# Fillings behind all scatters, three experts' weights split by GpSimd, and waits for single experts

## The chip, the cores and the metric

The kernel runs on one core of a Trainium2 chip. The time is that of the device for one execution, in microseconds (us); lower is better. The inputs are fixed in shape, and each execution computes the whole output.

## The reference

`x` has 4 x 512 tokens of 256 numbers. Three steps are computed:

```
x = x + 0.5 * ffn(layernorm(x))
x = x + attention(layernorm(x))
x = x + 0.5 * ffn(layernorm(x))

ffn(t):   shared = silu(t @ shared_gate) * (t @ shared_up) @ shared_down      # 256 wide
          each token goes to the 2 best of 16 experts by its router logits
          routed = sum over the 2 of weight * (silu(t @ gate_e) * (t @ up_e)) @ down_e   # 128 wide
attention: 16 heads of 128; q, k, v and the output weights are codes times scales of blocks of 32
```

Both FFNs use the same weights. The results are close to those of float32: most factors are split into a high and a low part, and a product is three matmuls (high x high, high x low, low x high).

## The kernel before

**Stages.** The first FFN takes from 0 to about 175 us, the attention with 64 heads (4 batches x 16; head u is one of them) until about 925, the second FFN the rest. The five engines run five programs written out by hand (`sync_program`, `pool_program` for GpSimd, `act_program` for ScalarE, `dve_program` for VectorE, `pe_program` for TensorE). Each engine runs its instructions in the order of its program; semaphores are the only tie between them. So the order of the lines is the schedule.

**Experts.** Both FFNs sort the token rows by expert in a DRAM buffer `xs_dram[f]` (f is 0 or 1). Each expert has a region of 2048 + 128 rows. `to_experts` (L605 on) scatters the normalized rows, one indirect DMA of 128 rows at a time, issued by GpSimd: 4 blocks q of 512 tokens, 2 choices k, 4 tiles i, 32 scatters for an FFN. Blocks 0 to 2 count on semaphore `scat0`, block 3 on `scat_3`. A tile of 128 rows is then read back, two tiles (a pair p, 24 pairs) at a time. The last tile of an expert reaches past its rows; there must be finite numbers there, since they go through a transpose by a matmul. For FFN 0 one indirect DMA, the **filling** (L643), writes 16 rows from each partition, 128 rows behind each expert's last one, with whatever is in `R`; its index `fill` is made by `behind()` on VectorE. For FFN 1 there is no filling: during the attention SyncE writes zeros from `in_empty` over all regions of `xs_dram[1]`, in PIECES x NE = 64 writes (L453, `empty_piece`), one or two behind each head from head 3 on.

**Tile loads.** SyncE's `tile_loads` (L481 on) takes the row offsets of the tiles from a table `toff` that VectorE has computed, in groups of 1, 3, 4, 4, ... pairs, and issues two loads of 128 KB for each pair (L502). Each group's words are loaded into registers and checked against bounds (L492). The first FIRST_RUN = 4 pairs hold tiles that are full after blocks 0 to 2, so they wait for `scat0` alone; ahead of pair 4 SyncE waits for `scat_3`, and in FFN 0 for `empty` and `fill0` (L487 to L491).

**The tiles.** For pair p TensorE transposes pair p + 1 (L1818), then multiplies pair p with gate and up (`product`, L1712 to L1714; the expert's number is read from a word in a register), transposes the hidden rows of pair p - 1 (L1843) and multiplies pair p - 2 with the down weights. ScalarE and VectorE take the results out of PSUM (L886, L898, L903, L909; L1368, L1380, L1392). VectorE also makes tables between them: `shifts` at p = 0, `needs` at p = 1, `in_tiles` from p = 2.

**Weights.** The FFN's weights come in NCHUNK = 18 pieces of 768 columns: 2 of the shared expert, then 16 experts. SyncE loads piece c into one of STAGES = 4 buffers (`chunk`, L433) and waits before it until c - 3 splits are done; all of these loads stand before `tile_loads(0)` in its program. ScalarE copies the high part (`split_hi`, L868) and VectorE subtracts it for the low part (`split_lo`, L1190, counted by `w_lo`). In `pe_program` every pair of FFN 0 waits for all 18 splits before its first product. For FFN 1 the split weights are prepared again during the attention and come from DRAM (`w_dram`, semaphore `e_in`).

**Attention.** A head's probabilities are turned by two DMA transposes (L464, `flip`, the two halves of a head), issued by SyncE as soon as the planes are written; GpSimd casts the turned planes (L683), and TensorE multiplies them with the values (L1949 on). The same queue of SyncE carries the loads of weight parts (L479), the loads and the write-backs of experts' weights (L514, L519) and the zeros.

Of the kernel before, what the change touches and what calls it, by code (L numbers as in the profile page):

```python
# [5 lines left out]
P = 128  # L6
F32 = mybir.dt.float32
# [15 lines left out]
KT = D // P  # L23
# [30 lines left out]

RESULTS = 3
# [28 lines left out]
SLOW_FROM = 9  # L84

# [47 lines left out]
class Views:  # L133
# [4 lines left out]
    "cst_in rw_in rw tri b_in bo_in bo bias w_hi w_lo e_in dv av pool_steps "  # L138
# [4 lines left out]
    "tt row behind need there blank fill0 gpos empty scat0 scat_3 toff0 toff1 "  # L143
# [7 lines left out]
def build(nc, t):  # L151
    with ExitStack() as ctx:  # L152
# [44 lines left out]
        m.xs_words = m.xs_dram[0].rearrange("n (d w) -> (n d) w", w=1)  # L197
# [5 lines left out]
        m.any_rows = R[:, O_XT:O_XT + NT * D].bitcast(F32)  # L203
# [105 lines left out]
def chunk_place(m, c):  # L309

    if c < SH_CHUNKS:
        return [m.Wsh[:, l, c * CH:(c + 1) * CH] for l in range(2)]
    return [m.We[:, c - SH_CHUNKS, l, :] for l in range(2)]
# [94 lines left out]
PIECES = 4  # L408
# [17 lines left out]
def sync_program(nc, sp, t, m, s):  # L426
# [4 lines left out]
    def chunk(c):  # L431
        wait(sp, s["w_lo"], c - STAGES + 1)
        sp.dma_start(m.stg[c % STAGES], t["ffn_w"][:, c * CH:(c + 1) * CH]).then_inc(m.staged[c % STAGES], 16)  # L433
# [14 lines left out]

    def empty_piece(i):

        e, n = i // PIECES, P // PIECES
        r0, rows = e * REGION + i % PIECES * (REGION // PIECES), REGION // PIECES
        sp.dma_start(m.xs_dram[1][r0:r0 + rows, :].rearrange("(p a) d -> p (a d)", p=n),  # L453
                     t["empty"][0:n, :]).then_inc(s["empty"], 16)
# [26 lines left out]
    def tile_loads(f):  # L481
# [4 lines left out]
        for group in GROUPS:  # L486
            if done == FIRST_RUN:  # L487
                sp.wait_ge(s["scat_3"], 16 * TOPK * QB * (f + 1))
                if f == 0:
                    sp.wait_ge(s["empty"], 16)  # L490
                    sp.wait_ge(s["fill0"], 16)  # L491
            _, words = nc.values_load_multi_w_load_instructions(  # L492
                m.toff[0:1, done:done + group], engines=[SP_ENGINE], min_val=0, max_val=(1 << 18) - 1)
            for p, word in enumerate(words, done):
# [8 lines left out]
                if p >= STORE_AT:  # L503
                    store(f, p - STORE_AT)
                    if f == 0 and p in PART_AT:
                        part(PART_AT[p])
# [30 lines left out]
    pieces = iter(range(PIECES * NE))  # L537
    for u in range(UNITS):
# [14 lines left out]
        if u >= EMPTY_FROM:  # L553
            for _, i in zip(range(2 if u % 3 == 0 else 1), pieces):
                empty_piece(i)
# [46 lines left out]
def pool_program(nc, pool, m, s):  # L602
# [31 lines left out]
    for q in range(QB):  # L634
        pool.wait_ge(s["xn_act0"], QB * (q + 1) - 2)
        pool.wait_ge(s["xn_dve0"], 2)
        pool.wait_ge(s["pos0"], q + 1)
        to_experts(0, q, 0)
        if q == QB - 1:

            pool.wait_ge(s["behind"], 1)
            pool.wait_ge(s["xt_hi0"], KT * QB)
            nc.gpsimd.indirect_dma_start(  # L643
                out=m.xs_words, out_offset=bass.IndirectOffsetOnAxis(ap=m.fill[:, 0:1], axis=0),
                in_=m.any_rows, in_offset=None).then_inc(s["fill0"], 16)
        to_experts(0, q, 1)
# [113 lines left out]
    for t in range(1, UNITS + 1):  # L760
# [22 lines left out]
        if t == 60:  # L783
            positions(0)
            pool.wait_ge(s["posp"], 1)
            pool.wait_ge(s["empty"], 16 * (PIECES * NE + 2))
            scatters(0, range(2))
# [17 lines left out]
    to_experts(1, 3, 1)  # L805

# [27 lines left out]
def act_program(nc, act, t, m, s):  # L834
# [28 lines left out]
    split = iter(range(NCHUNK))  # L863
# [16 lines left out]
    def tiles(f):  # L880
        for p in range(-1, NPAIR + 2):
# [23 lines left out]
            if 0 <= p - 2:  # L905
                b = (p - 2) % RESULTS
                act.wait_ge(s["r_dn"], NPAIR * f + p - 1)
# [189 lines left out]
def dve_program(nc, dve, m, s):  # L1097
# [86 lines left out]
    split = iter(range(NCHUNK))  # L1184

    def split_lo(count):
        for _, c in zip(range(count), split):
            hi, lo = chunk_place(m, c)
            dve.wait_ge(s["w_hi"], c + 1)
# [286 lines left out]
    split_lo(2)  # L1476
    shared_lo(0, 1)
    positions(0, 3, K0)
    split_lo(2)
    counted(0, CNT)  # L1480
    behind()
    tables(0)
    shared_add(0, 0)
    tables_row(0)
    counted_first(CNT)
# [196 lines left out]
    tables_row(1)  # L1682
    counted_first(CNT)
# [34 lines left out]
def pe_program(nc, pe, m, s):  # L1718
# [83 lines left out]
    def tiles(f, word):  # L1802
# [3 lines left out]
        for p in range(-1, NPAIR + 2):  # L1806
# [13 lines left out]
            if 0 <= p < NPAIR:  # L1820
                b = p % 2
                es = [expert(2 * p + j) for j in range(2)]
                if f == 0:
                    pe.wait_ge(s["w_lo"], NCHUNK)
                elif p == 0:
# [348 lines left out]
```

## Time and profile before

| | us |
|---|---|
| median of 3 runs | 1073.38 (1072.83 to 1074.72) |
| the profiled execution, time | 1076.45 |
| the profiled execution, span | 1074.7 |
| TensorE busy | 979.0 (91% of the span) |
| VectorE busy | 798.6 (74%) |
| ScalarE busy | 674.9 (63%) |
| GpSimd busy | 626.8 (58%) |
| DMA | 216.64 MB, mean 202 GB/s |

The span is from the first to the last instruction of the profiled execution; its time has what lies around it too. The page cuts the span into 40 slices of 27 us, in tenths:

```profile
PE   5549999899999999999999999999999997589995
DVE  7758567888887777787777777777787887368545
POOL 1750348776436877667787576687636378630252
PEclk9759999999999999999999999999999999879997
DMA  9867652778678887999999999999954468946653
```

A digit is the busy share of an engine in a slice (9 is 90% or more), in the row PEclk the TensorE clock that was granted, in tenths of full speed. TensorE has open time at the beginning (slices 0 to 2), where the first FFN begins, and around slice 34, where the attention ends and the second FFN begins.

### The profile page before, as it was taken

The page shows a single profiled execution, that of the slowest core. Times are in us where ns is not written, and L with a number is a line of the kernel's source. Part 1 is how long each engine was busy: PE and PEld are TensorE (multiplying, and loading weights), DVE is VectorE, ACT ScalarE, POOL GpSimd, SP SyncE. Part 2 cuts the span into 40 slices and gives each one's busy share as a digit, 9 for nine tenths or more (in the row PEclk, how much of TensorE's full clock was granted, in tenths as well). Part 3 has the DMA queues.
Part 4 walks back from the last instruction along what each step waited for, and adds up shares of the span by engine and source line. Part 5 has one row for each costly group of instructions (what it writes and reads, how often), then busy time and mean ns, then how long its engine had stood idle before and what let it go on. Part 6 is the DMA issues. An engine that isn't in the chain of part 4 may idle for free. (4 is left out here: it accounts for less than half of the span.)

```text
span 1074.7 us, 18907 instructions
## 1 busy us (share of the span) xinstructions
PE 979.0 (91%) x5314; PEld 839.1 (78%) x5314; DVE 798.6 (74%) x1679; ACT 674.9 (63%) x1485; POOL 626.8 (58%) x915
## 2 busy tenths in 40 slices
PE   5549999899999999999999999999999997589995
PEld 4449987577888888888787887888888885479984
DVE  7758567888887777787777777777787887368545
ACT  5535644767776767777676776777767765135631
POOL 1750348776436877667787576687636378630252
PEclk9759999999999999999999999999999999879997
DMA  9867652778678887999999999999954468946653
GB/s 308 288 247 218 211 186 69 162 184 186 141 163 205 218 172 184 250 263 234 199 225 252 263 275 198 261 223 233 214 110 82 79 141 203 388 173 190 191 173 102
DMA packets 331797, 216.64 MB, mean 202 GB/s; under 512 B 274352, under 2 KB 315952, under 8 KB 330160
## 3 DMA queue, kind: packets, MB, share of 16 engines
q1 hardware_dynamic: 325104, 191.31, 70.5%
q0 software_dynamic: 6288, 18.88, 5.4%
q10 hardware_dynamic: 304, 5.24, 1.4%
q8 instruction: 46, 0.75, 0.3%
q14 instruction: 55, 0.45, 0.1%
HBM read 108.96 MB, written 80.48 MB: 176 GB/s over the span
## 5 line engine op out<-in xcount | busy, mean ns | idle before, releaser
L683 POOL CAST R<-turned 128x512 fp32r<-128x512 f16 x512 | 289.6, 615 | 216.4 <-DMA turned<-work 149.0
L1712 PE MATMUL bank<-R 128*128 128x512 f32 (+2 forms) x1056 | 390.7, 370 | 22.9 <-DVE R L1353 11.4
L1713 PE MATMUL bank<-R 128*128 128x512 f32 (+2 forms) x1056 | 379.7, 360 | 0.0
L1714 PE MATMUL bank<-R 128*128 128x512 f32 (+2 forms) x1056 | 379.0, 359 | 0.0
L1712 PEld LDWEIGHTS bank<-R 128*128 128x128 f32 x1056 | 204.9, 194 | 57.6 <-DVE R L1353 12.9
L1714 PEld LDWEIGHTS bank<-R 128*128 128x128 f32 x1056 | 204.6, 194 | 28.2
L1713 PEld LDWEIGHTS bank<-R 128*128 128x128 f32 x1056 | 205.3, 194 | 26.7
L985 ACT ACTIVATE bank<-bank,soft 128x512 f32<-128x512 f32 x256 | 170.1, 666 | 70.4 <-DVE soft L1525 63.5
L1518 DVE SCALAR_TENSOR_TENSOR R<-bank,bias,R 128x512 fp32r<-128x512 f32 x192 | 143.9, 750 | 67.9 <-ACT R L1005 41.4
L1525 DVE TENSOR_REDUCE soft<-bank 128x1 f32<-128x512 f32 x256 | 168.6, 686 | 25.4 <-PE bank L1714 25.2
L1539 DVE SCALAR_TENSOR_TENSOR work<-bank,soft,work 128x512 f16<-128x512 f32 x256 | 185.3, 743 | 2.3 <-ACT work L998 2.3
L998 ACT ACTIVATE work<-bank,soft 128x512 f16<-128x512 f32 x256 | 161.3, 682 | 16.2 <-DVE soft L1533 13.5
L617 POOL DMA_INDIRECT R<-y_tiles,gpos x48 | 46.7, 974 | 125.6 <-ACT work L909 64.7
L1949 PE MATMUL bank<-R 128*128 128x512 f32 x256 | 104.7, 409 | 10.3 <-POOL R L683 7.7
L1950 PE MATMUL bank<-R 128*128 128x512 f32 x256 | 101.0, 395 | 0.0
L1951 PE MATMUL bank<-R 128*128 128x512 f32 x256 | 100.4, 392 | 0.0
L1005 ACT ACTIVATE R<-bank,bias 128x512 fp32r<-128x512 f32 x64 | 44.1, 689 | 82.5 <-PE bank L1951 82.4
L979 ACT ACTIVATE R<-bank,bias 128x512 fp32r<-128x512 f32 x128 | 86.9, 680 | 0.0
L609 POOL DMA_INDIRECT xs_dram<-work,pos x48 | 51.0, 1062 | 48.5 <-DVE pos L1229 34.8
L1966 PE MATMUL bank<-R 128*128 128x256 f32 x256 | 72.2, 282 | 3.4 <-DVE R L1518 3.4
L1968 PE MATMUL bank<-R 128*128 128x256 f32 x256 | 72.4, 283 | 0.0
L1967 PE MATMUL bank<-R 128*128 128x256 f32 x256 | 72.4, 283 | 0.0
(163 smaller groups left out, 1375.9 us busy)
## 6 DMA issues: line engine op xcount, KB each, us to landing
xs_dram<-in_empty SPq DMA_DIRECT2D x64, 544.0 KB, 5.5
work<-in_parts SPq DMA_DIRECT2D x64, 256.0 KB, 4.2
work<-in_ffn_w SPq DMA_DIRECT2D x34, 384.0 KB, 4.9
work<-xs_dram SPq DMA_DIRECT2D x96, 128.0 KB, 2.6
y_tiles<-work SPq DMA_DIRECT2D x48, 256.0 KB
w_dram<-work SPq DMA_DIRECT2D x16, 768.0 KB, 4.7
R<-w_dram SPq DMA_DIRECT2D x16, 768.0 KB
y_tiles<-in_empty ACTq DMA_DIRECT2D x2, 2176.0 KB
```

The costliest lines, as they stand in the source:

```text
L683: nc.gpsimd.tensor_copy(whole_into(m, l, kb), whole_block(m, u, l, kb)).then_inc(s["cast_pool"], 1)
L985: nc.scalar.activation(s_bank(m, qb)[:], s_bank(m, qb)[:], ACT.Exp, bias=m.mx[:, qb:qb + 1], scale=1.0, accum_out=m.sm[:, qb:qb + 1]).then ...
L998: nc.scalar.activation(m.planes[:, qb, 0, :], s_bank(m, qb)[:], ACT.Copy, scale=m.ri[:, qb:qb + 1])\
L1518: v_.scalar_tensor_tensor(out=dst[:, 1, :], in0=bank[bk][:], scalar=m.bias[:, which, h:h + 1], in1=dst[:, 0, :].bitcast(F32), op0=ALU.add, ...
L1525: v_.reduce_max(m.mx[:, qb:qb + 1], s_bank(m, qb)[:], AX_X, negate=True).then_inc(s["max"], 1)
L1539: v_.scalar_tensor_tensor(out=m.planes[:, qb, 1, :], in0=s_bank(m, qb)[:], scalar=m.ri[:, qb:qb + 1], in1=m.planes[:, qb, 0, :], op0=ALU.m ...
L1712: nc.tensor.matmul(out, ah, bh, start=(i == 0 and first), stop=False)
L1713: nc.tensor.matmul(out, ah, bl, start=False, stop=False)
L1714: last = nc.tensor.matmul(out, al, bh, start=False, stop=(i == n - 1))
L1949: nc.tensor.matmul(bank[1][:], vh, ph, start=(kb == 0), stop=False)
L1950: nc.tensor.matmul(bank[1][:], vh, pl, start=False, stop=False)
L1951: ins = nc.tensor.matmul(bank[1][:], vl, ph, start=False, stop=(kb == QB - 1))
```

## The change

Four things are changed.

1. **Filling behind the scatters.** In FFN 0 the filling goes from between the scatters of block 3 behind all of them. In FFN 1 the 64 zero writes go; in their place GpSimd issues a filling of its own (`fill1`) behind the last scatter, when all experts' weights have landed (it takes its numbers from their place). SyncE waits for it ahead of pair 4, as in FFN 0. `behind()` on VectorE goes behind `tables_row`, and FFN 1 has one too.
2. **GpSimd splits three experts.** The pieces of steps 14, 16 and 17 of the loads (experts 13, 14, 15; steps 14 and 15 are exchanged) are split by GpSimd, a copy and a subtraction each, behind the filling of FFN 0. ScalarE and VectorE split the other 15; VectorE does 12 of them before the tables, where it did 14. In SyncE's loads, step c still waits for c - 3 splits.
3. **Waits for own experts.** In FFN 0 TensorE waits, for pairs 0 to 7, for the count of splits that the experts of its two tiles need (a wait against a register), and from pair 8 for all. ScalarE and SyncE get a wait each, since a staging buffer lies where they write.
4. **Checks.** The offsets that SyncE takes from the table are no longer checked against bounds.

```diff
+POOL_STEPS = (NCHUNK - 4, NCHUNK - 2, NCHUNK - 1)
+OWN_STEPS = tuple(i for i in range(NCHUNK) if i not in POOL_STEPS)
+CHUNKS = OWN_STEPS[:-1] + (NCHUNK - 3, NCHUNK - 4, NCHUNK - 2, NCHUNK - 1)
+SPLIT_BY = 8
...
-        m.xs_words = m.xs_dram[0].rearrange("n (d w) -> (n d) w", w=1)
+        m.xs_words = [xs.rearrange("n (d w) -> (n d) w", w=1) for xs in m.xs_dram]
-        m.any_rows = R[:, O_XT:O_XT + NT * D].bitcast(F32)
+        m.any_rows = [R[:, at:at + NT * D].bitcast(F32) for at in (O_XT, O_Z)]
...
 def chunk_place(m, i):
+    c = CHUNKS[i]
...
     def chunk(c):
         wait(sp, s["w_lo"], c - STAGES + 1)
-        sp.dma_start(m.stg[c % STAGES], t["ffn_w"][:, c * CH:(c + 1) * CH]).then_inc(m.staged[c % STAGES], 16)
+        sp.dma_start(m.stg[c % STAGES], t["ffn_w"][:, CHUNKS[c] * CH:(CHUNKS[c] + 1) * CH]).then_inc(m.staged[c % STAGES], 16)
...
                 sp.wait_ge(s["scat_3"], 16 * TOPK * QB * (f + 1))
-                if f == 0:
-                    sp.wait_ge(s["empty"], 16)
-                    sp.wait_ge(s["fill0"], 16)
+                sp.wait_ge(s["empty"], 32 if f else 16)
+                sp.wait_ge(s[f"fill{f}"], 16)
             _, words = nc.values_load_multi_w_load_instructions(
-                m.toff[0:1, done:done + group], engines=[SP_ENGINE], min_val=0, max_val=(1 << 18) - 1)
+                m.toff[0:1, done:done + group], engines=[SP_ENGINE], min_val=0, max_val=(1 << 18) - 1,
+                skip_runtime_bounds_check_because="the table ends at the spare tile")
...
                     if f == 0 and p in PART_AT:
+                        if PART_AT[p] == 0:
+                            sp.wait_ge(s["w_lo"], NCHUNK)
                         part(PART_AT[p])
...
-        if u >= EMPTY_FROM:
-            for _, i in zip(range(2 if u % 3 == 0 else 1), pieces):
-                empty_piece(i)
...
         to_experts(0, q, 0)
-        if q == QB - 1:
-
-            pool.wait_ge(s["behind"], 1)
-            pool.wait_ge(s["xt_hi0"], KT * QB)
-            nc.gpsimd.indirect_dma_start(
-                out=m.xs_words, out_offset=bass.IndirectOffsetOnAxis(ap=m.fill[:, 0:1], axis=0),
-                in_=m.any_rows, in_offset=None).then_inc(s["fill0"], 16)
         to_experts(0, q, 1)
+    pool.wait_ge(s["behind"], 1)
+    pool.wait_ge(s["xt_hi0"], KT * QB)
+    nc.gpsimd.indirect_dma_start(
+        out=m.xs_words[0], out_offset=bass.IndirectOffsetOnAxis(ap=m.fill[:, 0:1], axis=0),
+        in_=m.any_rows[0], in_offset=None).then_inc(s["fill0"], 16)
+
+    pool.wait_ge(s["w_lo"], len(OWN_STEPS))
+    for n, c in enumerate(POOL_STEPS):
+        hi, lo = chunk_place(m, c)
+        pool.wait_ge(m.staged[c % STAGES], 16 * (c // STAGES + 1))
+        nc.gpsimd.tensor_copy(hi, m.stg[c % STAGES]).then_inc(s["w_pool"], 1)
+        pool.wait_ge(s["w_pool"], n + 1)
+        nc.gpsimd.tensor_tensor(lo, m.stg[c % STAGES], hi.bitcast(F32), ALU.subtract).then_inc(s["w_lo"], 1)
...
-            pool.wait_ge(s["empty"], 16 * (PIECES * NE + 2))
...
     to_experts(1, 3, 1)
+    pool.wait_ge(s["behind"], 2)
+    pool.wait_ge(s["e_in"], 16 * NE)
+    nc.gpsimd.indirect_dma_start(
+        out=m.xs_words[1], out_offset=bass.IndirectOffsetOnAxis(ap=m.fill[:, 0:1], axis=0),
+        in_=m.any_rows[1], in_offset=None).then_inc(s["fill1"], 16)
...
-    split = iter(range(NCHUNK))
+    split = iter(OWN_STEPS)
...
+                if f == 0 and p == 2:
+                    act.wait_ge(s["w_lo"], len(OWN_STEPS))
...
     shared_mul(0, 1)
-    split_lo(2)
+    split_lo(1)
     shared_lo(0, 1)
     positions(0, 3, K0)
-    split_lo(2)
+    split_lo(1)
     counted(0, CNT)
-    behind()
     tables(0)
     shared_add(0, 0)
     tables_row(0)
+    behind()
     counted_first(CNT)
     split_lo(NCHUNK)
     tiles(0)
...
     tables_row(1)
+    behind()
     counted_first(CNT)
...
-                if f == 0:
+                if f == 0 and p < SPLIT_BY:
+                    for e in es:
+                        pe.wait_ge(s["w_lo"], pe.snap(e + (SH_CHUNKS + 1), min_val=SH_CHUNKS + 1, max_val=NCHUNK))
+                elif f == 0 and p == SPLIT_BY:
                     pe.wait_ge(s["w_lo"], NCHUNK)
-                elif p == 0:
+                elif f == 1 and p == 0:
                     pe.wait_ge(s["e_in"], 16 * NE)
```

## Rows read from the trace of the kernel before

**Rows 1.** Busy time in a stretch of the attention (clock, DMA share, GB/s last).

```profile
340.00:750.00 410.00, 407.25 (x1989) 342.08 (x1988) 319.85 (x535) 296.17 (x661) 298.31 (x460) 1.00 0.95 228
```

**Rows 2.** Timeline of SyncE's queue in the attention: start, us, what, count.

```profile
342.43 4.13 SPq L464 DMA_TRANSPOSE turned<-work  x2
...
571.38 1.21 SPq L453 DMA_DIRECT2D xs_dram<-in_empty  x2
574.35 9.06 SPq L464 DMA_TRANSPOSE turned<-work  x2
...
587.32 5.58 SPq L464 DMA_TRANSPOSE turned<-work  x2
...
599.19 4.95 SPq L464 DMA_TRANSPOSE turned<-work  x2
...
610.17 5.62 SPq L464 DMA_TRANSPOSE turned<-work  x2
...
788.13 4.76 SPq L464 DMA_TRANSPOSE turned<-work  x2
```

**Rows 3.** TensorE's timeline, first FFN: start, us, what [idle before <- what ended it].

```profile
73.74 1.11 PE L1818 MATMUL bank<-cst,work 128*128 128x128 f32 x4 [7.23 <-DMA work<-xs_dram]
...
83.48 0.38 PE L1712 MATMUL bank<-R 128*128 x1 [1.12 <-DVE R L1392]
...
84.34 0.60 PE L1818 MATMUL bank<-cst,work 128*128 128x128 f32 x4
```

**Rows 4.** Busy time from pair 4 to the end of the tiles.

```profile
84.00:146.00 62.00, 61.80 (x519) 60.53 (x518) 42.74 (x108) 37.50 (x86) 10.69 (x12) 1.00 0.64 196
```

**Rows 5.** GpSimd's timeline, first FFN: filling and last scatter.

```profile
62.39 3.30 POOL L643 DMA_INDIRECT xs_dram<-R,fill  x1 [0.30 <-issue]
...
69.79 0.96 POOL L609 DMA_INDIRECT xs_dram<-work,pos  x1 [0.30 <-issue]
```

**Rows 6.** The filling (L643): from its start to landing, min/median/max.

```profile
DMA to landing us min/median/max: 10.5/10.5/10.5
```

**Rows 7.** Busy time while the filling flows (DMA share, GB/s last).

```profile
66.00:76.00 10.00, 2.77 (x14) 2.37 (x13) 1.17 (x2) 1.69 (x3) 4.38 (x6) 0.50 0.96 342
```

**Rows 8.** SyncE's tile loads, pairs 0 to 3; landing of those until 92.

```profile
L502 SPq DMA_DIRECT2D work<-xs_dram x8: 3/644/1199, 63.3 to 70.6; - x8
...
DMA to landing us min/median/max: 2.1/4.0/7.6
```

**Rows 9.** VectorE's timeline, first FFN: the last four splits.

```profile
61.31 3.54 DVE L1190 TENSOR_TENSOR R<-work,R 128x768 fp32r<-128x768 f32 x4
```

**Rows 10.** SyncE's last four loads of weights, first and last start.

```profile
L433 SPq DMA_DIRECT2D work<-in_ffn_w x4: 328/328/328, 52.1 to 55.8; - x4
```

**Rows 11.** SyncE ahead of pair 4: the table's words, then the first loads.

```profile
L492 SPq TENSOR_LOAD <-toff x1: 317/317/317, 75.8 to 75.8; - x1
...
L502 SPq DMA_DIRECT2D work<-xs_dram x2: 333/334/336, 77.8 to 78.4; - x2
```

**Rows 12.** Groups by shape, GpSimd: the splits of experts' weights in the attention.

```profile
L700 POOL TENSOR_TENSOR work<-work 128x768 fp32r<-128x768 f32 x16 | 29.5, 1847 | 1.3
...
L698 POOL CAST work<-work 128x768 fp32r<-128x768 f32 x16 | 13.3, 829 | 0.0
```

**Rows 13.** Timelines of GpSimd and of VectorE around 156 us.

```profile
156.26 0.76 POOL L675 TENSOR_TENSOR R<-work,R 128x256 fp32r<-128x256 f32 x1
...
156.46 0.58 DVE L1166 SCALAR_TENSOR_TENSOR ln<-ln 128x4 f32<-128x4 f32 x1
...
157.46 0.16 DVE L1166 SCALAR_TENSOR_TENSOR ln<-ln 128x4 f32<-128x4 f32 x1
```

**Rows 14.** FFN 1: last scatter, SyncE's loads from pair 4, TensorE's pair 4.

```profile
958.71 0.96 POOL L609 DMA_INDIRECT xs_dram<-work,pos  x1 [0.31 <-issue]
...
L502 SPq DMA_DIRECT2D work<-xs_dram x3: 332/333/887, 964.1 to 965.2; - x3
...
974.94 0.49 PE L1818 MATMUL bank<-cst,work 128*128 128x128 f32 x3
```

More of the change, by code:

```diff
@@ L137 @@
 SEMAPHORES = (
-    "cst_in rw_in rw tri b_in bo_in bo bias w_hi w_lo e_in dv av pool_steps "
+    "cst_in rw_in rw tri b_in bo_in bo bias w_hi w_lo w_pool e_in dv av pool_steps "
     "pre_in pre_mul pre_out "
@@ L142 @@
     "lg0 lg1 lg_sb rk_sb l_read0 l_read1 hot0 hot1 e2 rank0 rank1 cnt pos0 pos1 posp "
-    "tt row behind need there blank fill0 gpos empty scat0 scat_3 toff0 toff1 "
[1 row of a table added]
     "gu silu h h_hi h_lo dn x_add "
@@ L306, with chunk_place @@
 TABLE = (COUNT[1], COUNT[1] + NPAIR + WORDS)
-def chunk_place(m, c):
+def chunk_place(m, i):
+    c = CHUNKS[i]
     if c < SH_CHUNKS:
@@ L407 @@
 EMPTY_FROM = 3
-PIECES = 4
 def part_of(kind, g, hh):
@@ L447, in sync_program @@
     sp.dma_start(m.xs_dram[0][SPARE:XROWS, :], t["empty"][:, 0:D]).then_inc(s["empty"], 16)
[L449 to L454, printed above, removed]
     def empty_spare():
@@ L536, in sync_program @@
     sp.wait_ge(s["sh_out"], 16)
-    pieces = iter(range(PIECES * NE))
     for u in range(UNITS):
@@ L1182, in xt_lo @@
             .then_inc(s[f"xt_lo{ph}"], 1)
-    split = iter(range(NCHUNK))
+    split = iter(OWN_STEPS)
     def split_lo(count):
@@ L1188, in split_lo @@
             hi, lo = chunk_place(m, c)
-            dve.wait_ge(s["w_hi"], c + 1)
+            dve.wait_ge(s["w_hi"], OWN_STEPS.index(c) + 1)
             v_.tensor_tensor(lo, m.stg[c % STAGES], hi.bitcast(F32), ALU.subtract).then_inc(s["w_lo"], 1)
```

1 row of the table SEMAPHORES is left out of this document.

## The prediction

> **What bounds the kernel now.** I read first the busy time by stretch. In most of the attention TensorE is busy 407.25 of 410 us at full clock, with the DMA engines 0.95 busy [rows 1], so only work that holds TensorE up counts there. I then took the DMA queue's own timeline, because each head starts with a DMA transpose. From the head that starts at 342.43 to the one that starts at 788.13 there are 40 heads, 445.7 us; a usual head takes 10.98 us (599.19 to 610.17), 40 of them 439.2 us. So 6.5 us are lost in these 40. They are lost in few places: behind 574.35 the next head comes after 12.97 us. There the transposes occupied the queue for 9.06 us, right behind two emptying writes at 571.38 [rows 2]. Five heads lose something (at 507, 574, 643, 688 and 755 us): 1.3, 2.9, 1.5, 0.6 and 0.2 us. In each the transposes occupy the queue for longer than usual, GpSimd's casts are late, and TensorE waits for them.
>
> The second place is the start of the first FFN's tiles, in TensorE's timeline. Pair 1 is transposed only at 73.74 after 7.23 us of waiting for its load; pair 4 at 84.34 [rows 3]. From there to 146 TensorE is busy 61.80 of 62 us [rows 4], so a start that comes earlier is kept to the end of the stage, and what follows hangs on that end. Why is pair 1 late? GpSimd issues the filling at 62.39, between the scatters of the last block, and four scatters follow until 70.75 [rows 5]. The filling lands 10.5 us after its start, at 72.9 [rows 6]; between 66 and 76 the DMA engines are 0.96 busy [rows 7]. The loads of pairs 0 to 3 are issued from 63.3 to 70.6 [rows 8] and land in that crowd.
>
> **The change, part by part.** *1. Filling behind the scatters (FFN 1).* The four scatters now come first: 62.39 + 4 x 1.265 = 67.45. The filling is generated 67.45 to 70.75 (3.30 us [rows 5]) and its data flow after that, no longer beside the loads of pairs 0 to 3.
>
> When are these loads issued? Two fewer splits precede the tables on VectorE, 2 x 0.885 us by the four that take 3.54, and the fill's index moves behind them; before, the table was ready just ahead of these four, at 60.9 [rows 9]; now it is some 2 us earlier. But SyncE gains nothing by it: its last two weight loads, at steps 16 and 17, wait for the 13th and 14th split. Before, these were done by 55.8 [rows 10]. Now they come behind the tables: I put the table at 58.9, 1.0 us of index and counts behind it, then two splits, until 61.7. Then come two weight loads, and the first tile load is at 63.4 to 64.3 (63.3 before), pair 1 some 1.5 us behind, at 65 to 65.8. Of the landing times the least is 2.1 and the median 4.0 [rows 8]; I take 3, as the only company are the two weight loads and scatters: pair 1 at 68.5, against 73.74. By that, TensorE would be at pair 4's place at 84.34 - 5.2 = 79.1.
>
> Pair 4's load waits for the filling. Its data now move alone: 2.1 MB at the rate of [rows 7], 342 GB/s, are 6.1 us, so it lands at about 76.9 (bounds: 76.0 at a faster rate, 77.95 by the 10.5 us of [rows 6]). Before, the release was at 75.8 and the first load at 77.8 [rows 11]; 2.0 us in which the table's words are loaded and checked. The change drops the checks: I take 0.7 (bounds 0.4 to 2.0). First load 77.6, second 0.6 behind, landed 2.1 to 3 later, 80.3 to 81.2: say 80.6. So the filling, not pair 1, becomes the last wait: a gain of 3.7 instead of 5.2.
>
> *2. GpSimd's three splits.* One costs 0.83 + 1.85 us [rows 12], three with their waits 8.4: from 70.8 to 79.3, on an engine that has then nothing to do until the first gather of results. They are in time: the pairs go through the experts in order, and 13 to 15 (first ready at 73.6, 76.4, 79.2) come in pairs 5 to 7, multiplied from 82 on. VectorE and ScalarE do three fewer, which were not last there.
> They do have company. Where GpSimd runs a two-input instruction of 256 columns at 156.26 until 157.02, VectorE's instruction with two SBUF inputs started at 156.46 takes 0.58 us, until 157.04, instead of the 0.16 of the same one at 157.46 [rows 13]: it waits until GpSimd's ends. In the new place three of 1.85 us run beside VectorE's `shifts` and `needs`, whose end releases pair 0's down product; that product was already 1.12 us late [rows 3], and TensorE reaches pair 4 right after it. A block moves the 79.1 out; its first 1.5 us are hidden by pair 4's load. I take 1.85 us (one instruction; bounds 0 and 3.7, two): some 0.3 us are lost, and pair 4 is at 81.0. **Parts 1 and 2: -3.4 us**, bounds -5.2 and -1.5.
> The Trainium skill, page "SBUF — State Buffer", section "Who interferes with whom", says that such a pair of instructions contends for one read interface; its summary says the second blocks until the first ends. The trace agrees with its 157.02 and 157.04; by the rule at its worst the parts give the -1.5 of the bound, without it -3.7.
>
> *3. Waits for the own experts.* TensorE waits twice for each of pairs 0 to 7. Alone it gains nothing, since VectorE reaches the tiles only behind its own splits (62.6); it is what keeps pair 0 from waiting for GpSimd's 79.3. The trace shows no register-valued wait of TensorE. A gain is excluded, since instructions are added alone; at the other end SyncE's handling of four words (2.0 us [rows 11]) gives 0.5 us for each of 16, 8 us if none was hidden. I take 0.1: pairs 0 to 3 wait for pair 4's load anyway, and behind them the queue is ahead of the array (61.80 of 62 [rows 4]).
>
> *4. No emptying in the attention.* 64 writes of 544 KB go, 35 MB, and with them most of the backlog ahead of the transposes; weight loads and write-backs of experts' weights stay. I take the whole 6.5 us less 0.1: **-6.4 us**. Bounds: -6.6, and -3.6 if the worst head kept its loss, since its 12.97 us stand right behind both kinds [rows 2].
>
> *5. Filling in FFN 2.* The last scatter is issued at 958.71 [rows 14]; the filling would follow at 960.0. It lands at 969.4 (3.3 + 6.1) to 970.5 (10.5). Before, pair 4's load went at 964.1 [rows 14]; now 0.7 behind the filling, 970.1 to 971.2, second 0.6 later, landed 2.1 to 3 later: 972.8 to 974.8. TensorE is at pair 4 at 974.94 [rows 14]. What hides it are pairs 0 to 3 and VectorE's `needs`, by 0.1 to 2.1 us. All weights must have landed too; they are issued before the last block's scatters. VectorE has three small instructions more (0.65 us) where it afterwards waits. I take **+0.1**, bounds 0 and +1.5.
>
> **Sum:** -3.4 + 0.1 - 6.4 + 0.1 = -9.6. The profiled execution took 1076.45 with a span of 1074.7; it becomes 1066.9 with a span of 1065.1. The median of the three runs is 1073.38; less 9.6 it is **1063.8 us**.
>
> **Rivals.** *A, locks and late loads eat FFN 1's gain.* VectorE's tables instructions meet two or three of GpSimd's 1.85 us, or pair 1 lands at 71: -1.5 instead of -3.4, with +1 in FFN 2 instead of +0.1: 1066.6. For it speaks [rows 13]; against it that pair 4's load hides a part. *B, the attention's late transposes are not due to the emptying.* Weight loads and write-backs stay in these heads: the 6.4 stay, 1070.2. For it: other heads stand behind two emptying writes and lose nothing; against it: the queue was longest occupied right behind a full load of all kinds, of which these writes are the largest part [rows 2]. *C, the change doesn't do what it says*: an early pair has an expert of GpSimd's and TensorE waits until 79.3 all the same. The first product, now at 74.4 (0.7 behind pair 1), comes 4.9 later: +4.9 - 6.4 + 0.1, 1072. Against it: tiles come in expert's order, eight of them before pair 4. *D, slower.* Both tile streams now stand at pair 4 until the filling lands. If each filling took d longer than the 10.5 us of [rows 6], FFN 1 would give d - 2.6 (landing at 77.95, pair 4 at 81.7), FFN 2 d - 0.1; with -6.4 from the attention the sum 2d - 9.1 is above +2.1 from d = 5.6 on; at d = 7 it is +4.9, 1078.3. Against it: that landing was measured in a crowd, and now the engines are idle around it.
>
> **Chances.** Forecast 0.66, A 0.15, B 0.11, C 0.04, D 0.04. A measurement of this kernel tells some 0.2% (2.1 us) from no change: faster 0.92 (forecast, A, B), same 0.04 (C), slower 0.04 (D). The forecast's own range is 1061.6 (-5.2 - 6.6) to 1066; the one for 8 in 10 takes in A and, for part 4's bound of -3.6 beside it, reaches to 1068.5, and below to 1060.5, since emptying writes stand behind heads ahead of 342 too, which I counted at nothing.
>
> **What the profile after would show.** Pair 1's transposes near 68.5 and pair 4's near 81, with the wait there on its load or on VectorE's L1392 before it; SyncE's last two weight loads near 61 and 62; GpSimd's splits ending near 79; all heads between 342 and 788 at 10.98 us and a DMA share clearly below 0.95; the second filling landing by 970.5 and no wait of TensorE at FFN 2's pair 4. Wrong would be: slow heads that remain, a filling that lands later than 78, or gaps between the products of pairs 4 to 7.

## The result and the profile after

| | before | after |
|---|---|---|
| median of 20 runs each, us | 1074.4 (1069.65 to 1077.15) | 1071.24 (1067.84 to 1074.66, one outlier of 3727.68 aside) |
| the profiled execution, time (span) | 1076.45 (1074.7) | 1067.94 (1066.1) |

The ratio of the times is 0.9969 (95% interval 0.9957 to 0.9981): **3.3 us faster, where 9.6 were predicted**, and outside the predicted range. The two profiled executions differ by 8.5 us. That overstates the change: the one of before is near the slowest of its 20 runs, that of after near the fastest of its own.

I call this chip A. The later runs were on three faster chips (before: medians of 1050.8, 1049.0 and 1050.2), together called B, but for the last three, on a chip like A (before: 1076.4), which goes as A too. Each ratio below is to before on the same chip.

The profile after, with the lines that answer to those of before. First the busy time by stretch, as in [rows 1], [rows 7] and [rows 4] (clock, DMA share, GB/s last):

```profile
340.00:750.00 410.00, 409.84 (x2014) 347.11 (x2013) 323.77 (x543) 300.68 (x671) 303.25 (x467) 1.00 0.74 166
66.00:76.00 10.00, 7.92 (x38) 7.17 (x38) 5.14 (x10) 4.12 (x7) 9.14 (x9) 0.62 0.83 319
84.00:146.00 62.00, 61.22 (x505) 59.58 (x505) 40.29 (x102) 36.65 (x85) 11.79 (x14) 1.00 0.67 202
```

The attention's DMA share has gone from 0.95 to 0.74, and TensorE's open time in these 410 us from 2.75 to 0.16. The timeline of SyncE's queue has the same 40 heads as [rows 2]:

```profile
340.24 4.78 SPq L463 DMA_TRANSPOSE turned<-work  x2
...
571.37 5.91 SPq L463 DMA_TRANSPOSE turned<-work  x2
...
582.35 4.74 SPq L463 DMA_TRANSPOSE turned<-work  x2
...
780.25 4.72 SPq L463 DMA_TRANSPOSE turned<-work  x2
```

The 40 heads take 440.01 us instead of 445.70, 10.98 from 571.37 to 582.35 and nearly so elsewhere. The first FFN in TensorE's timeline, as [rows 3]; then VectorE and GpSimd beside each other:

```profile
67.94 1.12 PE L1828 MATMUL bank<-cst,work 128*128 128x128 f32 x4 [0.79 <-DMA work<-xs_dram]
...
77.59 1.08 PE L1828 MATMUL bank<-cst,work 128*128 128x128 f32 x4 [2.83 <-DMA work<-xs_dram]
81.74 0.60 PE L1828 MATMUL bank<-cst,work 128*128 128x128 f32 x4
```

```profile
68.03 0.96 POOL L639 DMA_INDIRECT xs_dram<-R,fill  x1 [0.31 <-issue]
...
72.59 1.84 POOL L649 TENSOR_TENSOR R<-work,R 128x768 fp32r<-128x768 f32 x1
...
72.75 1.74 DVE L1269 SCALAR_TENSOR_TENSOR runs<-runs,tab 128x48 f32<-128x48 f32 x1
```

The view of the filling's line alone gives its landing, as in [rows 6]:

```profile
DMA to landing us min/median/max: 9.2/9.2/9.2
```

Pair 1 is 5.8 us earlier, pair 3 (the line of 77.59) waits 2.83 us for its load, and pair 4 is 2.6 us earlier, without a wait for its own load. VectorE's L1269 takes 1.74 us beside GpSimd's subtraction; it took 0.21 before. The filling lands 9.2 us after its start, at 77.3. Pair 3's two loads are issued at 68.21 and 69.62, so they are under way beside it.

In the second FFN TensorE waits before pair 1 and before pair 0's products, and the two waits are longer than before. The first windows are of that stretch in after, the last line is of before:

```profile
952.91 0.63 PE L1828 MATMUL bank<-cst,work 128*128 128x128 f32 x4 [1.85 <-DMA work<-xs_dram]
956.20 0.58 PE L1722 MATMUL bank<-R 128*128 x1 [2.66 <-issue]
...
969.62 0.60 PE L1828 MATMUL bank<-cst,work 128*128 128x128 f32 x4
```

```profile
954.00:958.00 4.00, 1.80 (x8) 1.81 (x9) 3.15 (x6) 2.68 (x5) 0.00 (x0) 0.54 1.03 344
958.00:962.00 4.00, 4.00 (x24) 4.00 (x23) 1.08 (x6) 0.38 (x1) 0.00 (x0) 0.61 0.49 154
```

```profile
962.00:966.00 4.00, 3.80 (x20) 3.80 (x21) 2.67 (x9) 1.08 (x3) 0.00 (x0) 0.62 0.40 108
```

From pair 0 to pair 4 it takes 19.2 us; before it was 16.0. The filling is issued at 950.90 and lands at 959.1; the DMA engines are full beside it, and TensorE, after its waits, has a clock of 0.54 and 0.61 (its lower level of 1.2 GHz is 0.5) until 962. Before had a slow stretch there too, 0.62 over four microseconds. The difference is mostly waiting: TensorE's waits of over half a microsecond between pairs 0 and 4 add up to 6.2 us, before to 3.8.

### The profile page after: what moved, and what is told of

Read it like the earlier page. It is cut to its first block and busy times, and to the rows that moved or that the text cites. A ratio compares the mean times of both kernels' runs of the same rounds, so it can differ in the third digit from the quotient of the medians.

```text
span 1066.1 us, 18770 instructions
## 1 busy us (share of the span) xinstructions
PE 982.0 (92%) x5314; PEld 845.6 (79%) x5314; DVE 797.4 (75%) x1679; ACT 672.8 (63%) x1482; POOL 633.8 (59%) x922
## 5 line engine op out<-in xcount | busy, mean ns | idle before, releaser
L994 ACT ACTIVATE bank<-bank,soft 128x512 f32<-128x512 f32 x256 | 170.3, 667 | 70.5 <-DVE soft L1534 67.1
L606 POOL DMA_INDIRECT xs_dram<-work,pos x48 | 50.1, 1044 | 49.0 <-DVE pos L1238 35.5
```

Of the source, the lines that this page charges most:

```text
L994: nc.scalar.activation(s_bank(m, qb)[:], s_bank(m, qb)[:], ACT.Exp, bias=m.mx[:, qb:qb + 1], scale=1.0, accum_out=m.sm[:, qb:qb + 1]).then ...
```

## The experiments

Stage times of all profiled executions, in us, read from the starts of TensorE's transposes (L1818 and its like) and of SyncE's transposes. "40 heads" is the stretch of [rows 2]; "heads 0 to 12" ends where it begins; "second start" is from pair 0 to pair 4 of the second FFN, "second rest" from pair 4 to pair 23.

| kernel | chip | pair 1 | pair 4 | pair 23 | heads 0 to 12 | 40 heads | second start | second rest |
|---|---|---|---|---|---|---|---|---|
| before | A | 73.7 | 84.3 | 138.4 | 154.0 | 445.7 | 16.0 | 54.6 |
| before_fourth | A | 73.7 | 84.7 | 138.4 | 154.4 | 446.5 | 16.6 | 54.4 |
| after | A | 67.9 | 81.7 | 136.4 | 153.7 | 440.0 | 19.2 | 54.3 |
| after_fourth | A | 79.5 | 90.3 | 143.9 | 154.3 | 440.5 | 18.8 | 55.0 |
| after8 | A | 68.4 | 81.1 | 136.4 | 154.5 | 439.8 | 18.8 | 54.4 |
| before_again | B | 68.8 | 80.0 | 133.2 | 153.4 | 445.7 | 13.6 | 53.2 |
| before_third | B | 71.5 | 82.3 | 135.5 | 154.1 | 444.1 | 13.6 | 53.2 |
| after_again | B | 66.6 | 81.8 | 135.4 | 155.4 | 440.0 | 13.6 | 53.2 |
| after_third | B | 66.7 | 79.1 | 133.9 | 155.7 | 440.5 | 13.7 | 53.3 |
| empt_only | B | 68.5 | 79.9 | 133.1 | 154.6 | 441.1 | 13.7 | 57.0 |
| ffn1_only | B | 66.3 | 78.5 | 132.7 | 155.7 | 447.6 | 13.7 | 53.2 |
| fill1_added | B | 70.7 | 81.2 | 134.4 | 153.9 | 445.9 | 15.0 | 57.0 |
| fill0_back | B | 71.5 | 81.3 | 134.9 | 155.3 | 441.8 | 13.7 | 53.5 |
| no_pool_split | B | 65.8 | 79.5 | 135.3 | 154.6 | 441.7 | 13.6 | 53.2 |
| empt_nocheck | B | 69.9 | 80.4 | 133.6 | 153.6 | 440.5 | 13.7 | 53.2 |
| empt_store8 | B | 69.1 | 80.0 | 133.2 | 153.7 | 439.4 | 15.6 | 54.9 |
| best8 | B | 70.5 | 81.2 | 134.4 | 153.6 | 440.5 | 13.7 | 53.2 |

**First: the halves of the change, and both kernels again.** Theory S says that the first trace of before lost more than usual, theory G that a gain is given back at the second FFN's start. before_again is the kernel before unchanged, after_again the changed one.

> The kernel before once more, against itself, for a second trace of it. Theory S (spread: the trace of before that was shown lost more in the attention than a usual execution does): the 40 heads between head 12 and head 52 take some 442 us instead of the 445.7 of the first trace, and the span is about 1072. Theory G (gain given back: the loss in the attention is there in every execution, and the change gives most of it back where the second FFN starts): again 445 to 446 us, span near 1074.7. Both: ratio 1.000 within its interval.

> The changed kernel once more. Theory S: heads 12 to 52 take 439.5 to 441 us, as in the first trace of after (440.0 from transposes to transposes), while the span is nearer to 1069 than to 1066; the difference lies in the last heads, the start of the second FFN or its tail. Theory G: heads 12 to 52 near 440, the start of the second FFN 3 us slower between its table and pair 4 than in before. Ratio 0.997, as in the twenty runs.

empt_only is before with the zeros gone and the second filling in (parts 4 and 5):

```diff
-        if u >= EMPTY_FROM:
-            for _, i in zip(range(2 if u % 3 == 0 else 1), pieces):
-                empty_piece(i)
...
     to_experts(1, 3, 1)
+    pool.wait_ge(s["behind"], 2)
+    pool.wait_ge(s["e_in"], 16 * NE)
+    nc.gpsimd.indirect_dma_start(
+        out=m.xs_words[1], out_offset=bass.IndirectOffsetOnAxis(ap=m.fill[:, 0:1], axis=0),
+        in_=m.any_rows[1], in_offset=None).then_inc(s["fill1"], 16)
```

> The kernel before with part 4 and 5 alone: no zeros written in the attention, a filling behind the last scatter of the second FFN; the first FFN as before. Theory S: ratio 0.998 to 0.999 (-1 to -2 us), the heads 12 to 52 at 440. Theory G: -6 us in the heads, +3 behind them, ratio 0.997. By the prediction on record (-6.3): ratio 0.994.

ffn1_only is the changed kernel with the zeros back and that filling out, the same lines the other way.

> The changed kernel with its first FFN (filling behind the scatters, GpSimd's three splits, own experts' waits, no checks), but with the zeros still written in the attention and no filling in the second FFN. By the prediction on record -3.3 us, ratio 0.997; by the first trace of after, where pair 4 came 2.6 us earlier and the tiles' end 2.0, ratio 0.998. Theory S leaves that standing; theory G needs it at 0.997 or below, since the rest would then be given back.

Measured, as ratios to before with their intervals: before_again 0.9999 (0.9985 to 1.0013), after_again 0.9954 (0.9938 to 0.9971), empt_only 0.9969 (0.9955 to 0.9984), ffn1_only 0.9997 (0.9982 to 1.0012). So the first FFN's parts (1 to 3, and the checks left out) bring 0.3 us, with 1.6 either way, and not 3.3; parts 4 and 5 bring 3.3. Theory S falls for the attention: the 40 heads lose 6.5 us by the same kind of place in another trace, such as the transposes at 569.13, of 8.08 us, with the next ones 11.98 us behind:

```profile
569.13 8.08 SPq L464 DMA_TRANSPOSE turned<-work  x2
581.11 3.36 SPq L464 DMA_TRANSPOSE turned<-work  x1
```

Where the zeros are gone, the 40 heads take 439.4 to 441.8 us in eleven traces; where they are kept, 444.1 to 447.6 in six. That is part 4's mechanism, shown. But empt_only's trace gave back 3.8 us, in the second FFN's rest: 57.0 instead of 53.2.

**Second: what gives back, and which piece of the first FFN does what.** fill1_added is before with the second filling alone, zeros kept (the lines with + above).

> The kernel before, with the second FFN's filling added and the zeros kept, so that this filling is all that differs. Theory P (its price is the prediction's +0.1): within 0.5 us of before, pair 4 of the second FFN without a wait for its load. Theory G (the filling gives back 2 to 3 us of what the attention gains, which would explain why the version with part 4 and 5 alone gained 3.3 us and not the 5.6 us that its heads gained): +2 to +3 us, with a wait of TensorE at the second FFN's tiles that before has not.

It measured 1.0017 (0.9999 to 1.0036), 1.8 us slower than before, and its second rest is 57.0 too. So the filling, not the missing zeros, brings the stall. (Its pair 4 also waits 1.05 us for its own load; the filling took 9.41 us to land there, 8.12 in empt_only.) Its mechanism stands in empt_only's timelines of SyncE, ScalarE and TensorE, and then in the busy time during and behind the stall:

```profile
936.28 26.79 SPq L501 DMA_DIRECT2D work<-xs_dram  x24
963.12 0.42 SPq L473 DMA_DIRECT2D y_tiles<-work  x1
...
966.19 0.60 ACT L909 ACTIVATE work<-bank 128x512 f32<-128x512 f32 x1 [3.34 <-DMA y_tiles<-work]
...
968.35 0.38 PE L1713 MATMUL bank<-R 128*128 x1 [2.02 <-DVE R L1368]
```

```profile
964.00:968.00 4.00, 2.33 (x20) 2.09 (x19) 1.27 (x5) 1.64 (x4) 0.00 (x0) 1.00 0.66 219
968.00:972.00 4.00, 3.65 (x18) 3.66 (x19) 3.02 (x9) 1.85 (x4) 0.00 (x0) 0.60 0.85 232
```

SyncE issues the 24 tile loads of pairs 0 to 11 ahead of its first store of a result. Those from pair 4 wait for the filling, so the store goes out 8.6 us behind TensorE's pair 4 (954.52) instead of 1.6 (958.35 and 956.79 in before_again). ScalarE has three result buffers and waits 3.34 us for the store to land, TensorE waits 2.02 behind it, and its clock is 0.60 in the four microseconds that follow: 2.0 us of waiting and 1.8 in the tiles behind it, which is about what that clock costs.

empt_nocheck is empt_only without the checks of the table's words:

```diff
-                m.toff[0:1, done:done + group], engines=[SP_ENGINE], min_val=0, max_val=(1 << 18) - 1)
+                m.toff[0:1, done:done + group], engines=[SP_ENGINE], min_val=0, max_val=(1 << 18) - 1,
+                skip_runtime_bounds_check_because="the table ends at the spare tile")
```

> Before with parts 4 and 5 and with the bounds checks left out, the first FFN otherwise as before. The release of pair 4 to its first load took 2.0 us before and 0.6 in the changed kernel: pair 4 of the first FFN comes up to 1.4 us earlier if its load is the last wait. 1 to 1.5 us faster than the version with parts 4 and 5 alone (about 4.5 below before) if so; equal to it (3.3 below before) if SyncE's handling is hidden.

It measured 0.9959 (0.9944 to 0.9973), 4.3 us below before; the second rest is 53.2. The gain comes where I had not looked for it: not at the first FFN's pair 4, which stays at 80.4, but in the second FFN. From the filling's landing to the first store, with two groups of words between, it takes 10.1 us instead of 13.7. That brings the store to 5.3 us behind pair 4, and there the stall is gone. The two traces differ by 3.8 us in this stage, the times of the two versions by only 1.0 (on two chips, with intervals that overlap); so how often the stall occurs isn't shown. After has left the checks out too, and its store goes out 0.8 us behind pair 4.

fill0_back is the changed kernel with the first filling, and `behind()`, back in their old places (the part of the change's diff around them undone).

> The changed kernel with the first FFN's filling (and its index) back between the scatters of block 3; all else stays. If the filling behind all scatters makes pair 4 late (theory L: the landing of 8 to 9 us stood beside four scatters before and now stands alone at the end), pair 4 is transposed 1.5 to 2 us earlier than in the changed kernel and the whole is 1 to 2 us faster than it: 6 us below before. If it brought a gain, as the prediction has it (3.4 us with part 2), this is 2 us slower than the changed kernel: 2.5 us below before.

no_pool_split is the changed kernel with `POOL_STEPS = ()`, `CHUNKS = OWN_STEPS` and 14 splits ahead of the tables again.

> The changed kernel with all 18 splits on ScalarE and VectorE in the order of before; the filling stays behind all scatters, the waits for single experts stay. VectorE's instruction of 1.74 us beside GpSimd's subtraction should be back at 0.21. If the locks cost the first FFN its gain, this is 1 to 2 us faster than the changed kernel; if pair 4 stands at its load in any case (prediction: 0.3 us lost), it is within 0.5 us of it, or slower by the two splits that VectorE has again ahead of the tables (1.8 us).

They measured 0.9978 (0.9968 to 0.9988) and 0.9973 (0.996 to 0.9986). fill0_back has pair 1 at 71.5 again, 5 us late, and yet pair 4 at 81.3: theory L's earlier pair 4 did not come. Its 2.3 us below before are what the other branch had expected (2.5); but no changed kernel ran beside it on that chip, and its interval overlaps those of after_again and after_third, so a gain by the filling's place isn't shown by it. no_pool_split is 2.8 us below before. In it the lock is gone, L1269 takes 0.21 us, and pair 4 stands at its load, 3.12 us:

```profile
70.79 0.21 DVE L1269 SCALAR_TENSOR_TENSOR runs<-runs,tab 128x48 f32<-128x48 f32 x1
...
79.47 0.88 PE L1828 MATMUL bank<-cst,work 128*128 128x128 f32 x3 [3.12 <-DMA work<-xs_dram]
```

```profile
80.00:84.00 4.00, 4.00 (x20) 3.78 (x19) 0.93 (x2) 1.21 (x3) 0.00 (x0) 0.51 0.66 175
```

Behind that wait the clock is 0.51 from 80 to 84 (second fence). The tiles behind pair 4 take 2.6 us more than 53.2, and pair 23 is no earlier than in after_again. An earlier pair 1 alone thus only moves the wait: here to pair 4, in after to pair 3 (2.83 us), in after_again to pair 2 (3.28 us, until 73.57, where the filling lands at 73.25). It costs its length and a slow clock behind it.

**Third: the store's place.** empt_store8 is empt_only, best8 is empt_nocheck, after8 the changed kernel, each with one line changed:

```diff
-STORE_AT = 11
+STORE_AT = 8
```

> The version with parts 4 and 5 alone (checks kept), with STORE_AT 8 in place of 11: SyncE stores pair 0's result behind the load of pair 8, not of pair 11. Theory Q (what gives back 3.8 us in the second FFN is SyncE's queue: the first store stands behind all loads that wait for the filling, 8.6 us behind the place of pair 4 instead of 1.6, ScalarE's eviction waits for a result buffer, and TensorE loses a stall of 2.0 us and some of its clock behind it): the first store goes out 3 us or more earlier, the stall of 2.0 us at pair 6 or so is gone, pair 4 to pair 23 of the second FFN take 53.2 us instead of 57.0, and the whole is up to 3.8 us faster than before less 3.3. Rival (the stall comes from the loads of the tiles themselves, or from a slow clock): the stage stays at 57.0.

> Parts 4 and 5, no bounds checks, STORE_AT 8, the first FFN in the order of before. Theory Q: without checks there was no stall any more (53.2 us), so this equals the version with STORE_AT 11 and no checks: 4.3 us below before. If the store's lateness still costs in other executions of that version, it is up to 1.5 us faster than it.

> The changed kernel once more, for a third pair of traces. If pair 4 of its first FFN is always set by the filling behind all scatters, it stands at 81 to 82 again and the attention's 40 heads take 440 us again; 3.3 to 4.8 us below before.

> The kernel before once more. If its first trace, with pair 4 of the first FFN at 84.34, was an unusual one, this shows 80 to 81, as the four other traces with the first FFN of before do; if it is the usual one on some chips, 84. Its attention loses 6.4 us in the 40 heads again.

empt_store8 measured 0.9954 (0.9939 to 0.9969), best8 0.9931 (0.991 to 0.9951), after_third 0.9963 (0.9943 to 0.9983). With the checks kept, empt_store8's first store goes out 4.6 us behind pair 4, not 8.6, and no stall of ScalarE's eviction follows: this and empt_nocheck, two ways to an earlier store, speak for the queue as its cause. But the gain expected of it did not come in the trace. TensorE now waits 1.78 us for pair 4's own load, with some clock lost behind it; start and rest of the second FFN add up to 70.5 us against 70.7 in empt_only. The filling took 10.06 us to land in this trace, 8.12 in empt_only, and the load stands behind it; another execution need not have this wait.

after_third has pair 4 at 79.1, not at the 81 to 82 expected, with the heads (440.5) and the time (3.9 below before) as expected; before_third has it at 82.3, between the two values of its theories, and its heads lose 4.9 us, not 6.4.

best8 is the fastest kernel of the study by its median: 7.2 us below before, where the changed kernel is 3.9 and 4.8 below on the same kind of chip; the intervals overlap. It has neither GpSimd's splits nor the waits for single experts, and the first filling stays between the scatters. Its trace is no faster than empt_nocheck's, so whether its lead over that version is real stays open.

> The changed kernel with STORE_AT 8 in place of 11. Theory Q (also in the first FFN the stores stand behind the loads that wait for the filling; in three of its kernels with the filling behind all scatters ScalarE waited 1.65 to 2.3 us for a store near pair 8, and pairs 4 to 23 took 54.2 to 54.8 us instead of 53.2): pairs 4 to 23 take 53.2 us in both FFNs and no eviction waits for a store; 1 us faster than the changed kernel, 4.5 to 5.5 us below before. Rival (TensorE's waits for its own experts cost it): pairs 4 to 23 of the first FFN stay at 54 or more.

> The changed kernel once more: where pair 4 of its first FFN stands (79.0 to 81.8 so far), and how long head 0's transposes take to the first cast (11.2 us in two traces, 9.3 in the kernel before).

> The kernel before once more: pair 1 of its first FFN stood at 73.7, 71.5 and 68.8, pair 4 at 84.3, 82.3 and 80.0, so how late pair 1 comes changes from one execution to the next; this adds one to them. On the chip of the first pair of profiles (a span of 1070 or more) it tells whether 84.3 is usual there.

after8 measured 0.9994 (0.9966 to 1.0023), 0.6 us below before and not 4.5 to 5.5; its twelve times spread from 1069 to 1084. ScalarE no longer waited for a store in the first FFN, as expected (in after it waited 2.07 us near pair 8); but pairs 4 to 23 took 55.3 us, with the clock at 0.77 to 0.81 behind two waits of 2.06 and 1.51 us. The expected microsecond did not come; the store's lateness is real in the first FFN, but it isn't what decides there. Part of the 55.3 is what the rival of this experiment said, TensorE's waits for its own experts (about 0.4 us, see part 3 below). before_fourth has pair 1 at 73.7 and pair 4 at 84.7: both traces of before on chip A agree. after_fourth shows how far the changed kernel can fall: VectorE stood for 5.60 us, and TensorE got its first tile at 78.27:

```profile
63.78 0.69 DVE L1369 SCALAR_TENSOR_TENSOR X<-bank,X 128x512 f32<-128x512 f32 x1 [5.60 <-remote]
...
78.27 2.09 PE L1828 MATMUL bank<-cst,work 128*128 128x128 f32 x8 [20.24 <-DMA work<-xs_dram]
```

The releaser that the profile gives is "remote", no instruction of the kernel; TensorE, which writes the bank that L1369 reads, had stood still since 58.0. The five traces of chip A have such waits of 1 to 8.6 us, most of them around 940 and behind 1020, and the twelve of chip B have none above 1 us. The stages around them are where most of the 29.3 us lie by which the spans of before and before_again differ: 48.1 us against 36.8 from the last head's transposes to the second FFN's table, and 45.1 against 35.4 behind its pair 23, in before and before_again. What the waits are stays open.

## Why the prediction was wrong

**What failed.** Two terms of the sum. Parts 1 and 2 stood at -3.4, on the premise that the filling's data would move alone behind the scatters, no longer beside the loads of pairs 0 to 3; they moved beside the loads of pairs 2 and 3, and TensorE's wait went there. The term measured -2.0 in the two profiled executions, and with part 3 it measured -0.3 (-1.9 to +1.3) by the times of ffn1_only. Part 5 stood at +0.1, priced by pair 4's load alone; the traces show +2.6 in the second start on chip A and, on B, a stall of 3.8 where the checks are kept.

**Part 4 (-6.4).** Right: 6.0 us on chip A and about 5 on chip B in the 40 heads, at the places named. DMA share 0.74, all heads near 10.98.

**Parts 1 and 2 (-3.4).** The places came within a microsecond on chip A: pair 1 at 67.9 (68.5 predicted), filling landed at 77.3 (76.9), SyncE's last two weight loads at 60.1 and 61.0, pair 4 at 81.7 (81.0); only GpSimd's splits ended two microseconds early, at 77.1. For pair 4 that is luck: it was forecast to stand at its own load, behind the filling, but TensorE had already waited 2.83 us for pair 3's load and then worked with a clock of 0.64 from 77.6 to 81.6. The filling (68.03 to 77.28) and pair 3's loads (issued at 68.21 and 69.62) shared the DMA engines, which were 0.83 busy from 66 to 76. At pair 23 2.0 us of the 3.4 are left: near pair 8 ScalarE waits for a store. On chip B nothing is left: pair 23 stands at 133.9 on average over the seven traces with the first FFN of before, and at 134.0 over after_again, after_third and ffn1_only. On B the base failed too: how late pair 1 is before isn't fixed, and the 3.30 us of the filling are not what I took them for. One of GpSimd's indirect DMAs that starts beside VectorE's splits takes 3.30 to 3.33 us instead of 0.96. In before, before_fourth and before_third it is the filling; in before_again it is the scatter behind it:

```profile
59.30 3.54 DVE L1190 TENSOR_TENSOR R<-work,R 128x768 fp32r<-128x768 f32 x4
...
60.36 3.32 POOL L609 DMA_INDIRECT xs_dram<-work,pos  x1 [0.30 <-issue]
```

That is so in six traces with the first FFN of before, and in these pair 1 stands at 68.5 to 70.7; in the three where the filling is hit, at 71.5 to 73.7. (fill0_back has 71.5 as well: there a scatter ahead of the filling takes 2.79 us, and the filling lands late, at 70.0.) So the 3.30 us that I had called the filling's generation [rows 5] were VectorE's splits [rows 9]: the slow instruction ends 0.84 us behind them in all nine (here 62.84 and 63.68). The filling itself takes 0.96 in after, and its data took longer than my 6.1 us by about as much, beside the loads of pairs 2 and 3; the two errors cancelled. The Trainium skill, page "SBUF — State Buffer", section "Who interferes with whom", says that a DMA which seems stalled by VectorE is one whose descriptors GpSimd generates, starved of its port. The trace agrees, with 3.3 against 0.96 us. The same section says that a tensor_tensor of VectorE did not stall a DMA so; here the measurement decides, since L1190 is a TENSOR_TENSOR. I had used that section only for GpSimd's splits.

The lock of part 2 came as predicted (1.74 us beside 1.84) and cost little, by no_pool_split, which has no lock and pair 23 at 135.3, no earlier than the traces with one. But where GpSimd splits, heads 0 to 12 take 155.3 to 155.7 us on chip B, in four traces, against 153.4 to 154.6 in eight without. Most of it stands at the first head: GpSimd's first cast waits 3.38 us for the turned plane in after_third, 1.46 in before_third. On chip A it isn't there, and why it is on B stays open.

**Part 3 (+0.1).** No run undid these waits alone, but the traces show their place. Where nothing else holds TensorE, a pair takes 2.80 us from transposes to transposes. In fill0_back and after_again the steps behind pairs 4, 6 and 8 take 2.99 to 3.00, 2.97 and 2.84 to 2.88 us, and all from pair 9 on 2.80 again; the stage takes 53.6 us, where all seven traces of B without these waits have 53.2. The extra time stands between a pair's transposes and the next product, where the waits are; fill0_back first, then best8:

```profile
81.26 0.60 PE L1829 MATMUL bank<-cst,work 128*128 128x128 f32 x4
81.76 0.38 PE L1723 MATMUL bank<-R 128*128 x1
```

```profile
81.18 0.60 PE L1820 MATMUL bank<-cst,work 128*128 128x128 f32 x4
81.53 0.36 PE L1714 MATMUL bank<-R 128*128 x1
```

That makes about 0.4 us behind pair 4, an estimate from these steps; what the waits cost ahead of it isn't shown.

**Part 5 (+0.1).** Wrong on chip A: the second start takes 18.8 to 19.2 us instead of 16.0 to 16.6, **+2.6**, in all three traces. On chip B it is 13.6 to 13.7 with and without, but for two traces with the checks kept, fill1_added (15.0) and empt_store8 (15.6). I had asked only whether pair 4's load comes in time (in after it does, without a wait). What I missed is company: the 2 MB flow beside the loads of pairs 0 to 3, and in after TensorE waits 1.85 us for pair 1's. But that the filling makes the 2.6 us isn't shown. The longer wait is that before pair 0's products, 2.66 us in after, 3.88 in after_fourth and 3.80 in after8, and in the last two it stands behind one of VectorE's waits without a releaser:

```profile
962.64 1.29 DVE L1369 SCALAR_TENSOR_TENSOR X<-bank,X 128x512 f32<-128x512 f32 x2 [4.49 <-remote]
```

```profile
953.42 1.29 DVE L1369 SCALAR_TENSOR_TENSOR X<-bank,X 128x512 f32<-128x512 f32 x2 [3.07 <-remote]
```

before_fourth has such a wait too (3.06 us), and B has none. Pair 0 also comes earlier in the changed kernel: from the last head's transposes to pair 4 it is 71.7, 71.7 and 70.4 us against 69.8 and 70.2 in before, so 1.3 us are lost on average, not 2.6. I had also left out what is queued behind the waiting SyncE, the stores. In the traces of empt_only and fill1_added, with the checks kept, that costs 3.8 us; dropping them, which I had priced only as 1.3 us ahead of pair 4, is what saves this part.

**The sum.** The two profiled executions differ by -2.0 (to pair 23), -5.7 (40 heads), +1.9 (last head's transposes to pair 4 of the second FFN) and -2.9 (behind its pair 23), and +0.1 in all else: -8.6 of span, near the -9.6 predicted. But the -2.9 belong to no part of the change: before_fourth and after_fourth have this stretch 0.5 and 1.0 us shorter than before, the waits without a releaser fall in it, and on B it is 35.4 or 35.5 us in all twelve traces. So it is luck that this pair came near. With the stages above, -2.0 - 6.0 and +1.3 to +2.6 in the second start, some -6 us are left. The medians give 3.3. Executions like after_fourth, 8 us late in the first FFN, would make up such a difference, but the times alone don't show how frequent they are, so the last 2 to 3 us stay open. Of the rivals, B came nearest by its number (1070.2) and by luck, for the 40 heads refute its mechanism. A had the right places (its -1.5 for parts 1 and 2 and +1 for part 5). D had the second filling right and the mechanism wrong: it landed 8.2 us after its start, not late. C is refuted by pair 4 at 81.7. The upper end of the range, 1068.5, holds part 4's bound of -3.6 beside the forecast (1066.6) but not beside A (1069.4).

## What to carry to other kernels

Where a transfer is moved behind others to get it out of their way, look at what it meets in its new place, and at all that stands in its waiter's queue, stores included: here it met the loads of pairs 2 and 3, and in the second FFN the results' stores, queued behind the loads that waited, made the stall. One profile is one draw: before a stage's wait is booked as a gain, find what decides whether it occurs; here it was whether the filling or a scatter started beside VectorE's splits. Where TensorE waited 2.0 and 3.1 us (empt_only, no_pool_split), 3.8 and 5.7 us were lost in all, since the tiles behind the wait ran at 0.5 to 0.6 of the clock.

## What the runs showed of the hardware

An indirect DMA of GpSimd that starts beside back-to-back two-input instructions of VectorE is held up, in nine traces for 2.34 to 2.37 us, until 0.84 us behind the last of these. It isn't always held to their end: in after, beside three splits, one scatter took 1.06 and the next 1.44 us. The first ended 0.83 us behind the first split (60.08 and 60.91), the second 0.84 behind the last (61.82 and 62.66); after_fourth's filling took 1.75 us and ended 0.83 us behind the first of three (67.96 and 68.79). So the held-up DMA ended 0.83 to 0.84 us behind the end of one of the splits; what decides behind which isn't shown. Chips of one kind differ: the kernel before takes 1074 to 1076 us on A and 1049 to 1051 on B, and only A's traces have waits of over 1 us without a releaser.
